# Moving the second exponential and the input factors of the convolution kernel's setup from VectorE to GpSimd, ahead of its gathers

## What is computed

```
dt  = exp(log_dt)
A   = -exp(log_A_real) + 1j * A_imag
dtA = A * dt[:, None]
Ct  = Cc * (exp(dtA) - 1.0) / A
P   = dtA[:, :, None] * arange(length)
K   = 2.0 * einsum('hn,hnl->hl', Ct, exp(P)).real
```

## Time and profile before

| | us |
|---|---|
| median of three runs | 2086.11 |
| lowest, highest | 2084.29, 2087.57 |
| span of the profiled execution, from the first to the last instruction | 2084.3 |
| TensorE busy in the span | 2027.8 (97%) |
| VectorE busy | 1754.2 (84%) |
| ScalarE busy | 992.2 (48%) |
| GpSimd busy, DMA issues among it | 135.2 (6%) |

### The profile page before, as it was taken

The page is one execution under the profiler, slowest core; times in us unless marked ns, Lnnn a source line. Parts: engine busy times, 40 slices in busy tenths (PEclk is TensorE's granted clock), DMA queues, the critical chain, the costliest instruction groups (busy, mean ns, idle before and its releaser), DMA issues.

```text
span 2084.3 us, 33692 instructions
## 1 busy us (share of the span) xinstructions
PE 2027.8 (97%) x10192; PEld 1726.4 (83%) x10192; DVE 1754.2 (84%) x2204; ACT 992.2 (48%) x1255; POOL 135.2 (6%) x229
## 2 busy tenths in 40 slices
PE   3999999999999999999999999999999999999999
PEld 3998888878888788888888888888888888888887
DVE  8796999999999988778787779979788788767777
ACT  2222888878887533343343443453343343434332
POOL 3100000000000322210000020010000000000000
PEclk9999999999999999999999999999999999999999
DMA  6997999989999656754334996645334334368665
GB/s 246 336 343 282 353 352 359 359 339 352 359 354 340 168 164 198 196 143 109 91 101 114 341 316 210 205 144 129 94 101 110 91 106 106 96 215 306 198 209 187
DMA packets 247488, 459.51 MB, mean 220 GB/s; under 512 B 110534, under 2 KB 114822, under 8 KB 227718
## 3 DMA queue, kind: packets, MB, share of 16 engines
q1 hardware_dynamic: 230306, 416.03, 59.6%
q0 software_dynamic: 14944, 42.50, 6.7%
q10 hardware_dynamic: 2180, 0.26, 0.1%
HBM read 418.56 MB, written 63.73 MB: 231 GB/s over the span
## 4 chain that ended last, share of the span: by engine, by line
PE 86%; DVE 7%; issue 2%; DMA 2%; ACT 1%; POOLq 1%; DVEq 0%; POOL 0%; ACTq 0%; SPq 0%
PE ps L2323 19%; PE ps L2324 19%; PE ps L2325 19%; PE ps L2245 6%; PE ps L2247 6%; PE ps L2246 6%; PE ps L2217 5%; PE ps L2401 2%; PE ps L2402 2%; PE ps L2254 1%; DMA W<-in_w 1%; PE ps L2438 1%; PE ps L2439 1%; POOLq L750 1%; DVE part L1567 1%
## 5 line engine op out<-in xcount | busy, mean ns | idle before, releaser
L2323 PE MATMUL ps<-rows,oph 128*128 128x512 f32 x1196 | 467.3, 391 | 1.2 <-DVE opl L1659 0.6
L2324 PE MATMUL ps<-rows,oph 128*128 128x512 f32 x1196 | 466.9, 390 | 0.0
L2325 PE MATMUL ps<-rows,opl 128*128 128x512 f32 x1196 | 465.3, 389 | 0.0
L1567 DVE TENSOR_TENSOR part<-W,part 128x2048 fp32r<-128x2048 f32 x152 | 343.1, 2286 | 9.5 <-ACT part L919 8.9
L1662 DVE TENSOR_TENSOR tmp<-ps,tmp 128x512 f32<-128x512 f32 (+2 forms) x344 | 242.8, 707 | 106.9 <-PE ps L2402 61.4
L919 ACT ACTIVATE part<-W 128x2048 fp32r<-128x2048 f32 x152 | 290.6, 1915 | 70.8 <-DMA W<-in_w 47.9
L2325 PEld LDWEIGHTS ps<-rows,opl 128*128 128x128 f32 x1196 | 224.6, 188 | 47.7
L2323 PEld LDWEIGHTS ps<-rows,oph 128*128 128x128 f32 x1196 | 225.0, 188 | 45.6 <-DVE opl L1659 2.0
L2324 PEld LDWEIGHTS ps<-rows,oph 128*128 128x128 f32 x1196 | 225.0, 188 | 41.8
L2323 PE MATMUL ps<-th,wdh 128*128 128x512 f32 (+1 forms) x656 | 249.4, 380 | 1.5 <-DVE tl L1659 1.0
L2324 PE MATMUL ps<-tl,wdh 128*128 128x512 f32 (+1 forms) x656 | 248.7, 379 | 0.0
(11 more groups left out here) (246 smaller groups left out, 3028.0 us busy)
## 6 DMA issues: line engine op xcount, KB each, us to landing
W<-in_w SPq DMA_DIRECT2D x152, 1024.0 KB, 6.7
raw<-in_wgu SPq DMA_DIRECT2D x168, 256.0 KB, 2.8
traw<-kept_acts SPq DMA_DIRECT2D x78, 512.0 KB, 5.0
wraw<-in_wd SPq DMA_DIRECT2D x70, 512.0 KB
toep<-kpad SPq DMA_DIRECT2D x31, 1024.0 KB, 9.2
lraw<-picked_b SPq DMA_DIRECT2D x88, 256.0 KB, 4.1
kept_acts<-tmp SPq DMA_DIRECT2D x84, 256.0 KB, 2.4
urev<-in_urev SPq DMA_DIRECT2D x32, 256.0 KB, 7.1
```

What stands on the lines that cost most here:

```text
L1567: V.tensor_tensor(out=wl[c][:], in0=W[:, c], in1=wh[c][:].bitcast(F32), op=ALU.subtract).then_inc(w_lo, 1)
L2323: mm(to, lhsT=wh, rhs=mh, start=start, stop=False)
L2324: mm(to, lhsT=wh, rhs=ml, start=False, stop=False)
L2325: return mm(to, lhsT=wl, rhs=mh, start=False, stop=stop)
```

## The change

GpSimd gets a function state_factors ahead of its first gather. It waits for a new semaphore `dta_set`, computes the second exponential of `dta[:, 0]` in 128x64 tiles of its own (`eb`, `ebi`), waits for ScalarE's sines of the half angles, forms the factors without the division by |A| squared, writes them to `ct` and signals `factors_set`. [...] VectorE makes the half angles after announcing `dta`, then phases(0), quarter_turns(0) and the reciprocal, waits for `factors_set` and multiplies. round_turns becomes one instruction everywhere.

```diff
-CHUNK_LINKS = 12
+CHUNK_LINKS = 11
...
+            eb = sb(s, "eb", [P, 12, H])
+            ebi = sb(s, "ebi", [P, H], I32)
...
+            def state_factors():
+                made = [0]
+                def then(ins):
+                    made[0] += 1
+                    ins.then_inc(factor_link, 1)
+                    pool.wait_ge(factor_link, made[0])
+                n, r, q, em = (eb[:, i] for i in range(4))
+                one, x = ebi[:].bitcast(F32), dta[:, 0]
+                ar, ai, cr, ci, s2, c2 = ex[:, 6], par[:, 2], par[:, 3], par[:, 4], ex[:, 8], ex[:, 9]
+                def both(to, a, b, op):
+                    return pool.tensor_tensor(out=to, in0=a, in1=b, op=op)
+                pool.wait_ge(dta_set, 1)
+                then(pool.tensor_scalar(n, x, 1 / math.log(2), None, ALU.mult))
+                then(pool.tensor_scalar(n, n, MAGIC, -MAGIC, ALU.add, ALU.add))
+                then(pool.tensor_scalar(n, n, -126.0, 127.0, ALU.max, ALU.min))
+                pool.tensor_scalar(ebi[:], n, 127.0, float(2 ** 23), ALU.add, ALU.mult)
+                then(pool.tensor_scalar(r, n, -LN2_1, None, ALU.mult))
+                then(both(r, r, x, ALU.add))
+                then(pool.tensor_scalar(q, n, -LN2_2, None, ALU.mult))
+                then(both(r, r, q, ALU.add))
+                then(pool.tensor_scalar(q, r, 1 / 40320, 1 / 5040, ALU.mult, ALU.add))
+                for d in (720, 120, 24, 6, 2, 1):
+                    then(both(q, q, r, ALU.mult))
+                    then(pool.tensor_scalar(q, q, 1 / d, None, ALU.add))
+                then(both(q, q, r, ALU.mult))
+                then(both(q, q, one, ALU.mult))
+                then(pool.tensor_scalar(em, one, -1.0, None, ALU.add))
+                then(both(em, em, q, ALU.add))
+                then(pool.tensor_scalar(eb[:, 0], em, 1.0, -2.0, ALU.add, ALU.mult))
+                pool.wait_ge(half_sin, 1)
+                then(both(eb[:, 0], eb[:, 0], s2, ALU.mult))
+                both(eb[:, 1], eb[:, 0], s2, ALU.mult)
+                then(both(eb[:, 2], eb[:, 0], c2, ALU.mult))
+                then(both(eb[:, 1], eb[:, 1], em, ALU.add))
+                for k in range(2):
+                    both(eb[:, 8 + k], cr, eb[:, 1 + k], ALU.mult)
+                    then(both(eb[:, 10 + k], ci, eb[:, 1 + k], ALU.mult))
+                both(eb[:, 0], eb[:, 8], eb[:, 11], ALU.add)
+                then(both(eb[:, 1], eb[:, 10], eb[:, 9], ALU.subtract))
+                for k in range(2):
+                    both(eb[:, 8 + k], ar, eb[:, k], ALU.mult)
+                    then(both(eb[:, 10 + k], ai, eb[:, k], ALU.mult))
+                both(ct[:, 0], eb[:, 8], eb[:, 11], ALU.add)
+                both(ct[:, 1], eb[:, 9], eb[:, 10], ALU.subtract).then_inc(factors_set, 1)
+            state_factors()
             for s in range(SEQ // 2):
                 gather_inner(0, s, slice(0, SPLIT))
...
             def round_turns(t, before=0):
-                link(V.tensor_scalar_add(t, t, MAGIC), before)
-                link(V.tensor_scalar_add(t, t, -MAGIC), before)
+                link(V.tensor_scalar(t, t, MAGIC, -MAGIC, ALU.add, ALU.add), before)
...
             tt(dta[:, 1], ai, dt, ALU.mult)
+            V.memset(tick[:, 0:1], 0.0).then_inc(dta_set, 1)
...
+            (half angles as before, moved here, then half_arg)
             phases(0)
             quarter_turns(0)
-            expm1_of(dta[:, 0], ex[:, 0], ex[:, 1], ex[:, 2], exi[:, 0])
-            one = exi[:, 0].bitcast(F32)
-            tt(ex[:, 2], ex[:, 2], one, ALU.mult)
...
-            dve.wait_ge(half_sin, 1)
...
-            tt(ct[:], ex[:, 0:2], twice(ex[:, 10:11]), ALU.mult)
+            tt(ex[:, 10], ex[:, 4], ex[:, 5], ALU.add)
+            link(V.reciprocal(ex[:, 10], ex[:, 10]))
+            link(V.tensor_scalar(ex[:, 10], ex[:, 10], quarter[:, 2:3], None, ALU.mult))
+            dve.wait_ge(factors_set, 1)
+            tt(ct[:], ct[:], ex[:, 10:11].to_broadcast([P, 2, H]), ALU.mult)
             powers(0)
```

More of the change, by code:

```diff
@@ L333, in build @@
         dve_link = sem("dve_link")
+        factor_link = sem("factor_link")
+        dta_set = sem("dta_set")
+        factors_set = sem("factors_set")
         half_arg = sem("half_arg")
@@ L1439, in add_conv @@
                                 op=ALU.add).then_inc(x1_done, 1)
+            half, whole = ex[:, 10:12], ex[:, 4:6]
+            link(V.tensor_scalar(half, dta[:, 1:2].to_broadcast([P, 2, H]), 0.5, None, ALU.mult))
+            link(V.tensor_scalar(whole, half, 1 / TWO_PI, None, ALU.mult))
+            link(V.tensor_scalar_add(ex[:, 5], ex[:, 5], 0.25))
+            round_turns(whole)
+            for i, part in enumerate((TWO_PI_1, TWO_PI_2)):
+                link(V.scalar_tensor_tensor(out=ex[:, 8:10], in0=whole, scalar=-part,
+                                            in1=half if i == 0 else ex[:, 8:10], op0=ALU.mult, op1=ALU.add))
@@ L1441, in _ @@
+            link(V.tensor_scalar_add(ex[:, 9], ex[:, 9], math.pi / 2))
+            V.tensor_scalar(ex[:, 8:10], ex[:, 8:10], PI, -PI, ALU.min, ALU.max).then_inc(half_arg, 1)
             phases(0)
             quarter_turns(0)
-            expm1_of(dta[:, 0], ex[:, 0], ex[:, 1], ex[:, 2], exi[:, 0])
-            one = exi[:, 0].bitcast(F32)
-            tt(ex[:, 2], ex[:, 2], one, ALU.mult)
-            link(V.scalar_tensor_tensor(out=ex[:, 3], in0=one, scalar=-1.0, in1=ex[:, 2],
-                                        op0=ALU.add, op1=ALU.add))
@@ L1448, in _ @@
-            dve.wait_ge(half_sin, 1)
-            em, s2, c2, cr, ci = ex[:, 3], ex[:, 8], ex[:, 9], par[:, 3:4], par[:, 4:5]
-            twice = lambda a: a.to_broadcast([P, 2, H])
-            V.tensor_scalar_add(ex[:, 0], em, 1.0)
             V.tensor_tensor(out=ex[:, 4], in0=ar, in1=ar, op=ALU.mult)
             tt(ex[:, 5], ai, ai, ALU.mult)
-            link(V.scalar_tensor_tensor(out=ex[:, 0], in0=ex[:, 0], scalar=-2.0, in1=s2,
-                                        op0=ALU.mult, op1=ALU.mult))
```

## The result

The changed kernel takes **2106.72 us** (median of five runs, 2103.85 to 2110.47) against 2087.57 us for the kernel before on the same chip (five runs, 2084.29 to 2095.79): a ratio of 1.0094 with a 95% interval of 1.0077 to 1.0111, or 19.2 us more. The forecast was 2103.6 us in a range of 2091 to 2114, slower with 0.93.

What follows compares the result with a forecast made beforehand. TensorE, 97% busy, bounds the kernel, with GpSimd's queue to `tri` the later chain at the start. kernels(2) +14.8, clock +0.3 and +2.8, group 3 -0.4 sum to +17.5 us: 2103.6 us, range 2091 to 2114.

Steps and rivals of the forecast that it cites:

- The mechanism: At the start, factors ahead of GpSimd's gathers make `tri` late; `pk` waits for it, then TensorE waits before kernels(2).
- chain of factors, undisturbed: GpSimd's 42 instructions on 128x64 ahead of the first gather, at 0.17 or 0.25 us plus links: 11.3 us.
- added by mutual exclusion: GpSimd and VectorE instructions blocking each other during the chain; F taken midway between 20.3 and 28.5 us.
- factors done (F): End of GpSimd's chain of factors, where the gathers begin: 24.4 us, between 20.3 and 28.5.
- eight gathers: GpSimd's gathers between the factors and the memsets of `tri`: 29.6 us like the second eight, ends 26 and 36.
- `tri` later by: `tri`, behind factors and gathers on GpSimd, ready at 58.55 us instead of 43.09: 15.5 us later.
- clock and what VectorE's chain leaves of it: TensorE's slow clock after idling before kernels(2): kernels +0.3 us, 2.8 in all at the next kernels; ends 0 and 4.
- group 3 on: At group 3 the 0.37 us wait for kernels falls away by the merged rounding: -0.4 us.
- the third rival: VectorE and GpSimd fully exclude each other: F = 28.5 us, 4.1 us more, 2107.7 us; chance 0.25.
- the change helps as drawn: Gather steps short enough that `tri` comes before 43.7 us; at 2.0 us a step, 2081 us; chance 0.02.
- GpSimd is quick and undisturbed: F = 17.3 us and gathers of 26 to 28 us: 2090 to 2094 us; chance 0.15.
- An instruction of about 1 us: Each GpSimd instruction in the chain costs about 1 us: F = 51 us, `tri` at 85 us, 2131 us; chance 0.08.

Runs made afterwards that it cites:

- kernel 8: The kernel after, with GpSimd's chain of factors held back until VectorE is about to wait for it: 2114.48 us in one run.
- kernel 4: The kernel before, with the chain of factors added on GpSimd ahead of its gathers and its result unused: 2110.46 us, ratio 1.0116.
- kernel 6: The kernel after, with the memsets and select of `tri` right behind the factors, X first, and all 16 gathers behind them: 2084.08 us, ratio 0.9990.
- kernel 1: The kernel before, with the memsets, iotas and select of `tri` and `ident` put ahead of all gathers: 2088.21 us, ratio 1.0005.
- kernels 1 and 2: Kernel 1, and the kernel after with the same memsets, iotas and select put ahead of state_factors: the latter 2085.8 us, ratio 1.0006.
- round_only: The kernel before, with the merged rounding alone: 2083.92 us, ratio 0.9988.
- kernel 5: The kernel before, with the merged rounding, five gathers ahead of the memsets and select of `tri` and eleven behind, X first: 2078.87 us, ratio 0.9964.

## Why the prediction was right, and where it wasn't

**The mechanism** stands, step by step: `pk` waits 21.7 us (some 20 said), TensorE idles 21.3 us before kernels(2) (15 or more said), VectorE waits at `ct`, ge(0) gains nothing, and from 120 us on the distances are as before within 0.5 us. The sum was 17.5 us and came out at 19.6 by the trace and 19.2 by the medians. Its terms:

| term | predicted | measured |
|---|---|---|
| GpSimd may start | 8.95 | 9.13 |
| chain of factors, undisturbed | 11.3 | 16.5 |
| added by mutual exclusion | 4.1 | 1.9 |
| factors done (F) | 24.4 | 27.48 |
| eight gathers | 29.6 | 31.6 |
| memsets and select | 4.55 | 4.25 |
| `tri` later by | 15.5 | 20.3 |
| `pk` to kernels(2) | 18.1 | 18.04 |
| kernels(2) later by | 14.8 | 19.54 |
| clock and what VectorE's chain leaves of it | +3.1 | +0.72 |
| group 3 on | -0.4 | -0.62 |
| sum | 17.5 | 19.6 |

**The chain was priced 5.2 us too low.** I scaled the copy and the select down from 256 and 128 elements a partition, to 0.17 us for one input and 0.25 for two. The groups of GpSimd's instructions in the kernel after (busy time, mean ns of one, idle before) show how far off that was:

```profile
L834 POOL TENSOR_TENSOR eb<-eb 128x64 f32<-128x64 f32 x12 | 4.3, 360 | 0.9
L848 POOL TENSOR_SCALAR eb<-eb 128x64 f32<-128x64 f32 x6 | 2.4, 397 | 0.5
...
L853 POOL TENSOR_SCALAR eb<-eb 128x64 f32<-128x64 f32 x1 | 0.2, 242 | 0.1
```

Undisturbed (kernel 8) a two-input instruction takes 0.32 us and a one-input one mostly 0.37, more than with two inputs and not less; the forms of two operations that end in a multiplication or begin with one take 0.24. Counted as in the forecast that is 27 x 0.32 = 8.6 us, 5.4 us for the 15 others, and 33 links of 0.09: 17.0 us, less a little where two unlinked ones overlap, or the 16.5 measured. The rows that I scaled were of other operations, a copy and a select, and scaling them down to 64 elements gave half the price; whether the size or the operation misled me no run separates. The Trainium skill (GPSIMD Engine Reference, Engine selection) calls GpSimd about two times slower than VectorE with two inputs and roughly at line rate with one. The trace agrees with neither: 0.32 against VectorE's 0.22 us with two inputs, 0.37 against its 0.20 with one. It still agrees with the table's advice, to leave elementwise work to VectorE.

**The exclusion was priced 2.2 us too high.** Between nothing and 8.2 us I took the middle; kernel 8 says 1.9 us on GpSimd (18.35 - 16.5) and 0.4 us on VectorE (9.64 - 9.25). It is there, in single instructions of GpSimd's timeline of the kernel after:

```profile
11.03 0.93 POOL L841 TENSOR_SCALAR eb<-eb 128x64 f32<-128x64 f32 x1
```

This took 0.93 us for what takes 0.38 alone (kernel 8). It ran while VectorE made `mag` and `ang`, two-input work on 128x512. But GpSimd did not stand still for all of such work, as the third rival said: VectorE's four two-input instructions on 128x512 last 2.8 us in all, and GpSimd lost 1.9 us to everything that VectorE did. Where VectorE works to the end, in kernel 4, it is more, 2.6 us (19.1 - 16.5). That rival, at 2107.7 us, has the number nearest to the median and reached it with the wrong cause: its F of 28.5 us came from a cheap chain doubled by exclusion, where the chain is dear and hardly disturbed. Here the page's rule, an exclusive lock for the whole instruction (the Trainium skill, SBUF — State Buffer, Who interferes with whom), is borne out by GpSimd's memsets against casts and tensor_scalars of VectorE (2.92, 2.47 and 1.68 us), where the hold even lasted over several instructions in a row, and only in part by the factors' chain.

**The gathers** took 31.6 us. The steps beside the Toeplitz loads are 5.3 and 6.5 us long (33.90 to 39.19 to 45.68 us), the quiet ones 2.95 to 3.2, nearly as before; 29.6 was a fair reading, and the range's 26 to 36 held it.

**The clock was priced 2.4 us too high.** I charged the pair behind kernels(2) with what the first pair of the kernel took, 9.2 us. It took 7.0 (82.59 us to 89.64, where VectorE takes it up), against 6.29 before. The profile shows no low clock in those 9.2 us; windows of the kernel before (window, length, TensorE's busy time and count, clock, DMA share, GB/s):

```profile
36.00:38.00 2.00, 1.82 (x5) 1.00 0.89 272
...
41.00:43.00 2.00, 1.82 (x5) 1.00 1.02 410
```

The granted clock is 1.00 through the whole first pair (36.2 to 45.7 us), and in the kernel after the same pair took 6.60 us. What slowed it to 9.2 us is not shown. From kernels(2) to kernels(3) it is 21.80 us against 21.08. Windows of the kernel after (with all engines):

```profile
81.00:84.00 3.00, 2.47 (x20) 2.19 (x21) 2.18 (x5) 0.37 (x1) 1.08 (x2) 0.50 1.02 407
84.00:87.00 3.00, 3.00 (x14) 2.96 (x13) 0.00 (x0) 1.28 (x1) 1.08 (x2) 0.50 1.05 406
```

The granted clock is 0.50 (1.2 GHz) up to 87 us, in the first 5.5 us of work, and the 128 matmuls lose 20.88 - 18.59 = 2.3 us; the kernel before, with 1.75 us of idling, had lost 20.14 - 18.59 = 1.55 of it already.

So the two errors at the chain left 3.1 us too little, the gathers 2.0, and the clock 2.4 too much; small terms make up the rest of the 2.1 us between 17.5 and 19.6. The forecast is 3.1 us under the median, 1.5 us of it because I added the sum to 2086.11 us and the median of the kernel before became 2087.57. It was right in sign, place and mechanism. That the number came so near is partly luck: the chain's price was wrong by 5.2 us, and the exclusion and the clock, both priced too high, made up for 4.6 of them.

**ge(0)** was to come at some 27 us, barely before 28.5, and kernels(0) started at 30.32, 1.8 us after the one before. It follows from F, as does the first gather's issue, at 30.95 us where I had said 26.5. It costs nothing in the kernel after, and 2.9 us where nothing else is late (kernel 6).

**The other rivals.** That the change helps as drawn needed 2.6 us a step or less; none was under 2.9. That GpSimd is quick and undisturbed needed F at 17.3 us; the chain alone takes 16.5 us from 9.13. An instruction of about 1 us was the rule nowhere; the longest took 0.93.

## What to carry to other kernels

GpSimd is busy 7% of the span, and still work put in front of its queue cost 19 us. Before putting work in front of something on an engine, list what stands behind it in the same queue, and how late each may be. Here the cheap repair was the order itself: constants that somebody waits for go ahead of transfers that nobody needs soon, which was worth 7.5 us together with the merged rounding, without moving any work. It matters where they go: at the very start, as in kernel 1, they held VectorE up and gained nothing. And a chain of dependent small instructions costs GpSimd some 0.4 us an instruction at 128x64, and in this change a fused multiply-add of VectorE was written as two of them.

## What was not expected of the hardware

- **GpSimd's memsets hold casts and tensor_scalars of VectorE until they end, several in a row.** A 2x32 tensor_scalar took 2.92 us instead of 0.17 (kernels 1 and 2), a 128x32 cast 1.68 us in the kernel before and 2.47 in round_only. In each of these it ended with the memset of X, through several instructions of GpSimd. The select of `tri` did it too: a 128x512 tensor_scalar took 1.56 us instead of 0.49 (kernel 5), and 1.55 in kernel 6. The tensor_tensor beside the same select took its usual 0.42 us, and the two of 128x512 beside the memset of `tri` in kernel 5 their usual 0.67. The length of such a hold depends on when VectorE arrives, so a saving ahead of it can vanish, as that of the rounding did at `pk`.
- **One input is dearer than two** on GpSimd at 128x64: 0.37 us against 0.32 in kernel 8; of the forms of two operations some took 0.24, others 0.44.
- **The clock's price grows little with the idle time.** In the table, idle stretches of 0.6 to 2.9 us before kernels(2) cost the next 128 matmuls either nothing (18.59 us) or 1.6 to 1.7; those of 8 to 23 us cost 2.0 to 2.6. The same 2 to 3 us of idling went both ways: round_only at 2.86 us kept its clock, factors_no_queue at 2.10 us lost it (window, length, TensorE's busy time and count, clock, DMA share, GB/s). First the windows of round_only:

```profile
60.00:62.00 2.00, 1.54 (x21) 1.00 1.05 412
62.00:64.00 2.00, 2.00 (x16) 1.00 1.01 410
```

  Then those of factors_no_queue:

```profile
61.00:63.00 2.00, 2.00 (x20) 0.69 1.06 410
63.00:65.00 2.00, 2.00 (x10) 0.50 1.01 409
```

  These are single profiled executions, and what decides between the two cases stays open. It is part of why kernels 5 and 6 differ by 5.2 us in the time and by 2.9 at kernels(2).
